# Products with unused results on TensorE, in the sort and ahead of the experts, in a kernel of causal attention and a mixture of eight experts

## The reference

```
x = x + layernorm(attn(layernorm(x), Wc_down, Wq_up, Wkv_up, Wc_proj))     # x: 4 x 1024 x 256, 16 causal heads of 16
# ffn of the layernormed x, t tokens, E = 8 experts, d = 256, F = 1024:
assign = argmax(x @ centroids.T); onehot = one_hot(assign, E)
disp = onehot * x;  xn = layernorm(disp) * ln_g + ln_b
h = relu(xn @ W1 + b1);  y = disp + h @ W2 + b2;  out = sum over e of onehot * y
x = x + layernorm(ffn(layernorm(x), ...))
```

## Time and profile before

| | |
|---|---|
| runs | 911.83, 909.88, 913.42 us; median 911.83 |
| profiled execution | 911.0 us, of which the span from first to last instruction is 909.3 |
| mean granted clock of PE over the span | 0.952 |
| PE busy | 832.1 us (92%) |
| DVE busy | 660.1 us (73%) |
| ACT busy | 546.2 us (60%) |

### The profile page before, as it was taken

One profiled execution on the slowest core, in us unless ns is written; L12 is line 12 of the kernel. 1 busy time (PEld: TensorE's weight loads), 2 busy tenths in 40 slices (PEclk: granted clock), 3 DMA queues, 4 the chain that ended last, 5 costly groups with the idle time before them and its releaser, 6 DMA issues. The chain is left out here.

```text
span 909.3 us, 20322 instructions
## 1 busy us (share of the span) xinstructions
PE 832.1 (92%) x5520; PEld 497.5 (55%) x5521; DVE 660.1 (73%) x2204; ACT 546.2 (60%) x1206; POOL 292.2 (32%) x548
## 2 busy tenths in 40 slices
PE   7999999999999999999999959349999999999993
PEld 3533343333333334333333328249999999999993
DVE  7789889888898988879898316835666666666652
ACT  3625667766677777667677836115666555666651
POOL 4502323343234422342223330141334434333211
PEclk9967999999999999999999989659999999999998
DMA  6102223212221111211130019950010100100000
GB/s 198 49 31 72 80 90 107 96 56 74 95 74 43 49 33 58 65 40 40 55 118 30 22 54 317 294 192 19 29 35 30 35 28 30 36 31 19 17 25 1
DMA packets 55508, 62.88 MB, mean 69 GB/s; under 512 B 12910, under 2 KB 47110, under 8 KB 55312
## 3 DMA queue, kind: packets, MB, share of 16 engines
q1 hardware_dynamic: 51696, 53.67, 18.0%
q0 software_dynamic: 3744, 8.40, 2.9%
HBM read 35.86 MB, written 9.55 MB: 50 GB/s over the span
## 5 line engine op out<-in xcount | busy, mean ns | idle before, releaser
L762 ACT ACTIVATE PR<-bank 128x512 f32<-128x512 f32 (+1 forms) x512 | 257.7, 574 | 129.4 <-PE bank L676 127.2
L810 DVE CUSTOM_DVE_ANT_0 junk<-bank,causal 128x384 bf16<-128x384 f32 (+3 forms) x512 | 221.0, 487 | 32.5 <-PE bank L645 30.8
L645 PE MATMUL bank<-K,Q 96*128 96x512 bf16 (+3 forms) x768 | 225.0, 340 | 7.6 <-DVE R L782 5.4
L676 PE MATMUL bank<-Q,K 99*128 99x512 bf16 (+3 forms) x768 | 227.3, 333 | 4.7 <-ACT W1s L762 2.9
L813 DVE TENSOR_REDUCE MP<-bank 128x1 f32<-128x512 f32 x256 | 162.8, 682 | 16.4 <-PE bank L645 16.2
L943 POOL TENSOR_SCALAR_AFFINE_SELECT PR<-PR 128x512 f32<-128x512 f32 x96 | 61.1, 636 | 300.2 <-ACT PR L762 298.1
L1508 PEld LDWEIGHTS hp<-XNT,LT 128*128 128x128 f32 x1248 | 147.5, 194 | 4.8 <-DVE XNT L1580 2.9
L1508 PE MATMUL hp<-XNT,LT 128*128 128x128 f32 x1248 | 148.0, 278 | 2.2 <-DVE XNT L1580 2.2
L676 PEld LDWEIGHTS bank<-Q,K 99*128 99x128 bf16 x768 | 68.4, 98 | 146.3 <-ACT PR L762 63.1
L1516 PE MATMUL yp<-W2s,LT 128*128 x624 | 141.2, 379 | 0.7 <-DVE z L1592 0.7
L693 PE MATMUL bank<-PR,V 128*32 128x512 f32 (+2 forms) x1152 | 129.7, 535 | 0.2 <-ACT W1s L748 0.2
(11 more groups left out here) (190 smaller groups left out, 790.8 us busy)
## 6 DMA issues: line engine op xcount, KB each, us to landing
Q<-T SPq DMA_DIRECT2D x192, 64.0 KB, 2.6
W1s<-in_L_ffn_W_dram SPq DMA_DIRECT2D x8, 1024.0 KB, 5.9
W2s<-in_L_ffn_W_dram SPq DMA_DIRECT2D x8, 1024.0 KB, 10.3
Y<-in_L_attn_x_dram SPq DMA_DIRECT2D x8, 512.0 KB, 6.1
Y<-W1s SPq DMA_DIRECT2D x32, 128.0 KB
LT<-in_L_attn_x_dram SPq DMA_DIRECT2D x8, 512.0 KB, 5.8
x_rows<-LT SPq DMA_DIRECT2D x8, 512.0 KB, 5.6
W1s<-den_rows SPq DMA_DIRECT2D x15, 256.0 KB
```

The lines of the kernel that those rows point to most:

```text
L645: last = pe.matmul(bank[:, at:at + w], Q[0:NR, g, i // BW, h, i % BW * P:(i % BW + 1) * P], K[b % 2][0:NR, k * NQ:k * NQ + w], start=True, ...
L676: last = pe.matmul(dst[:, i, :], K[b % 2][0:KR, j * P:(j + 1) * P], Q[0:KR, g, c, h, off:NQ], start=True, stop=True)
L762: act.activation(PR[t % RB][:, heads[0]:heads[-1] + 1, off:NQ], unit_of(ST[(NU * n + u) % STB], s), ACT.Exp, scale=SCALE).then_inc(exp_don ...
L810: op = dve.tensor_tensor_reduce(junk[:, done % 2, at:at + w], src, causal[:, NQ - w:NQ], 1.0, LOWEST, ALU.add, ALU.max, dst)
```

## The change

In the sort PE gets 22 products of 128 columns of `ones` with 512 columns of `counts_q` (a table of small integers that is ready before), into a PSUM tile `idle` that nobody reads. Each waits for one of DVE's steps: four between the transposes of the parameters and `pfx` (steps 4, 6, 7 and 8 of `rt`), and 18 between `tot` and `slp` (steps 9 to 23, `eq_ready`, and the first two of `tables_ready`). At the head of `experts` PE gets 28 products of the 128 x 128 identity with itself, in 32-bit floats, without any wait, ahead of its wait for W2. No engine but PE gets or loses an instruction.

```
@@ route, the sort
+            idle = ps3("idle", [P, NQ])
@@ block.tensor
                 last.then_inc(par_t, 1)
+                def keep_warm(sem, count):
+
+                    pe.wait_ge(sem, count)
+                    pe.matmul(idle[:, :], ones[:, :], counts_q[:, 0:NQ // NT, :], start=True, stop=True)
+
+                pe.wait_ge(made, 8)
+                for k in (4, 6, 7, 8):
+                    keep_warm(rt, k)
                 pe.wait_ge(made, 7)
                 pe.wait_ge(oh_ready, 1)
                 oh = OH[:, :, :].rearrange("p t e -> p e t")
                 pe.matmul(pfx[:, :], below[:, :], oh, start=True, stop=True).then_inc(counts, 1)
                 pe.matmul(tot[:, :], ones[:, :], oh, start=True, stop=True).then_inc(counts, 1)
+                for k in range(9, 24):
+                    keep_warm(rt, k)
+                keep_warm(eq_ready, 1)
+                for k in (1, 2):
+                    keep_warm(tables_ready, k)
                 for t in range(NT):
@@ experts
+        idle = psum("idle2", [P, NQ])
@@ block.tensor
+            for _ in range(28):
+                pe.matmul(idle[:, 0:P], ident[:, :], ident[:, :], start=True, stop=True)
             pe.wait_ge(w2_in, 16 * E)
```

## The result

The changed kernel takes 913.2 us (median of 20 runs), the kernel before 910.37 us over as many. The ratio is 1.003, with a 95% interval of 1.0018 to 1.0043: 2.8 us slower, between 1.6 and 3.9. One run of each kernel stood far out (1229.3 and 1407.5 us); the medians include it, the ratio does not. By the bound of 0.5% this is no change; it is clear of its own noise all the same, and on the side I had not forecast. The profiled execution took 915.1 us, its span 913.4, against 909.3 before.

The account below looks back on a forecast made before the run. PE, busy in 92% of the span, was taken to bound the kernel, with a hole around the sort. Profiled 911.0 us, sort -1.2, `hp` 0, gives 909.8; the median lies 0.8 above: 910.6 us, range 907.8 to 912.9.

Parts of the forecast that it names:

- part 4: After `slp`: ACT waits for W1 and copies until 601.94, so at most 1.34 us of the sort's gain passes; 1.2 taken.
- Part 1: In the sort: four products ahead of `pfx` at the low clock make it and `cum` 0.28 us later; +0.3 us taken.
- Part 2: In the sort: 18 products between `tot` and `slp` cost nothing and raise the clock by about 587 us, though not surely.
- Part 3: In the sort: at the high clock an `slp` product takes 0.076 us, not 0.152; `slp` ends 2.2 us earlier, at 594.0.
- Rival 2: In the sort: the clock doesn't rise, or strided operands keep `slp` at 0.152 us; +0.3 us, 912.1, chance 0.23.
- the bound of 0.076: For `slp` at the high clock: time of one product and its load if it halves from 0.152 us.
- the load rule of the Trainium skill: A load of P columns takes P / 1.2 ns whatever the clock, 107 ns for 128; net gain 1.4 us, not 1.9.
- Part 5: Head of the experts: 28 products, 56 instructions, 6.3 to 8.4 us; the clock falls again before `hp`, so 0 won there.
- Rival 3: Head of the experts: the 28 products at a low clock take 11.9 us and delay `xp`; 2.3 us slower, 914.1, chance 0.06.
- the sign of rival 3: Head of the experts: an `xp` that starts the moment the 28 products end would show them in its way.

Follow-up runs that it names:

- after_fourth: The changed kernel without an edit, run again on the same chip as gather_late; ratio to the kernel before 0.9999 (0.9979 to 1.0020), median 910.9 us.
- head_only: The changed kernel without the 22 products in the sort, the 28 at the head kept; ratio to the kernel before 1.0002 (0.9986 to 1.0018), median 911.3 us.
- head_only_2: head_only once more, unchanged; ratio to the kernel before 0.9994 (0.9973 to 1.0015), median 909.5 us.
- gather_late: The changed kernel with the last three of POOL's eight first gathers held until `xp` is done; ratio to the kernel before 1.0016 (1.0002 to 1.0030), median 910.6 us.
- bridge: head_only with 34 products at the head and six more between the first transposes and the first `hp`; ratio to the kernel before 0.9993 (0.9974 to 1.0012).

## Why the prediction was wrong

The forecast was 1.2 us off the time of the kernel before, as no clear change: +0.3 for `pfx`, -1.5 from `slp` after the cap of part 4, 0 in `hp`. The mean stretch of the profiles went the other way, from 39.11 us (three profiles) to 40.69 (six), +1.6, at the lower end of the 1.6 to 3.9 first measured. By segment: +0.35 to `IDX`, -0.14 to `xp`, +1.69 to `hp`, -0.32 to the second `hp`. Two things thus carried the result off the forecast: the gain in `slp` that did not come, and a wait behind `xp` that the sum did not hold. The range missed the 913.2 by 0.3 us, which alone would say little: the median of the kernel before was 911.83 over the runs I had and 910.37 over 20. The sign is what was wrong.

*Part 1, `pfx` behind four products*: right. Forecast 0.28 us later behind DVE's first step, measured 0.29 (581.54 - 578.50 against 580.29 - 577.54), and +0.35 from `best` to `IDX`.

*Part 2, the clock in the sort*: right. It rises near 587.5 in the changed profile (0.94 over 587 to 592), the products cost DVE nothing, and `slp` waits 0.74 us for the last table.

*Part 3, `slp` at the high clock*: this is the step that failed. "I take it that cycles halve with the clock" is false for these strided operands. `slp` takes 4.85 to 4.92 us in all profiles with the tables as they were, and its pace is the same on both sides of the clock's fall. Rival 2's "or `slp` takes 0.152 us in any case because its operands are strided" was the truth, at a chance of 0.23 for the whole rival. Its time, 912.1, still lacks the wait behind `xp`. Neither the bound of 0.076 nor the load rule of the Trainium skill ("TensorE: Matmul & The Clock Gate", LDWEIGHTS) had to do with it: loads alone contiguous moved 0.147 to 0.133 us, and a pair at 0.064 us, load included, is below that rule's 107 ns.

*Part 4, the cap of 1.34 us by W1*: never tested, since nothing came earlier.

*Part 5, the 28 products*: the count was right, and the length, 8.3 to 9.4 us from a low start where I had 8.4. That the clock is at 0.50 again when `hp` begins was right in five of six profiles; in after_fourth it fell 1.0 us into it. The gain for the first `hp` was 0.3 us on average where I took 0. It was not a matter of course, as head_only, head_only_2 and gather_late show, in which the clock stayed high. What the part lacked, and the sum put at nothing, is a longer wait between `xp` and `hp`: 3.62 us on average against 1.93. I had let the 28 products matter only through their length and the clock. Rival 3 had them in the way of `xp`, and `xp` was not late by them (10.45 us behind `IDX` against 10.59). In the changed profile `xp` does start 0.14 us after the 28 end, which I had named as the sign of rival 3; but DVE's `XNf` ends at 607.93 us there, at the same moment, and `xp` starts 0.15 us behind it, as it did before (606.98 and 607.12). The late signal stands behind `xp`, and no rival held it.

What stays open is what makes the signal late. Seen is: it came in five of twelve profiles with a high clock at `xp` and in none of eight with a low one, and in bridge two of PE's own next instructions were held too. Not shown is what part the gathers have, why the same program has it in some executions only, and whether dense 32-bit products just before are needed or only the high clock they leave. Nor is the 2.8 us of the medians fully placed: the profiles hold 1.6 of it, and the two repeats of twelve runs showed 0.7 and -0.1 us.

## What to carry to other kernels

Before a clock is bought for a stretch, find in the trace whether its instructions get faster with it: here the stretch that cost 4.9 us was paced by its strided operands and gained nothing. Products that keep PE warm may come with more than a clock, so look at the first real dependency behind them, in several profiles, since what stands there may come in some executions only; and see where each profiled execution lies among its runs, as the fastest one does not stand for the others. And where runs scatter by more than the effect, measure one stretch between two fixed instructions: it told 0.3 us where medians of twelve runs could not tell 2.

## What the runs showed of the hardware

- A product of 78 strided columns of bf16 with strided weights (stride 64 bytes each) takes 0.147 us at the granted clocks 0.50 and 1.00 alike; at 0.50 it takes 0.133 us with contiguous weights, and 0.064 us with both contiguous.
- DVE writing 2048 columns of bf16 with a stride of 256 bytes takes 9.2 us where the contiguous write takes 1.2 (18.41 and 2.35 us for two).
- PE's signal behind a recorded end of work can come 2.8 to 3.3 us late (five profiles). The record of the instruction looks normal; only the wait of the engine behind it, named "remote" in the profile, tells:

```profile
DVE XNT L1598 <- remote: 2.5, 1, 2.5
```
